# Shared keys and values in the global attention of a hybrid layer, and a shorter neighbourhood chain

## The reference

```python
# 1: neighbourhood attention, 4 heads of 16, window 7x7, then an MLP
x = x + neighbourhood_attention(layernorm(x)) @ proj_w + proj_b     # softmax over 49 keys + rpb
x = x + gelu(layernorm(x) @ fc1_w + fc1_b) @ fc2_w + fc2_b
t = x as (2, 1024, 64)
# 2: global attention, 8 heads of width 64 each, no bias on q, k, v
a = ln(t)
q = (a @ Wq).reshape(b, t, h, e) * e**-0.25
k = (a @ Wk).reshape(b, t, h, e) * e**-0.25
v = (a @ Wv).reshape(b, t, h, e)
t = t + softmax(q k^T) v @ Wu + bu
# 3: a scan of 33 steps; each picks a weight set by an argmax over its state, most do nothing
t = t + scan(ln(t))
```

## Time and profile before

| what | us |
|---|---|
| timed runs | 797.28, 794.80, 792.45 (median 794.8) |
| span of the profiled execution | 796.3 |
| neighbourhood stage, first score to last projection | 26.6 to 177.8 |
| handover | 177.8 to 194.4 |
| global pairs 0, 1, 2, 3 | 106.1, 112.3, 112.2, 102.3 |
| end of pair 3 to the end of the program | 627.3 to 796.3 |
| busy: PE, DVE, ACT, POOL | 679.7, 525.6, 418.5, 30.5 |

### The profile page before, as it was taken

The page is one execution under the profiler, slowest core; times in us unless marked ns, Lnnn a source line. Parts: engine busy times, 40 slices in busy tenths (PEclk is TensorE's granted clock), DMA queues, the critical chain, the costliest instruction groups (busy, mean ns, idle before and its releaser), DMA issues.

```text
span 796.3 us, 11131 instructions
## 1 busy us (share of the span) xinstructions
PE 679.7 (85%) x3779; PEld 355.4 (45%) x3780; DVE 525.6 (66%) x1043; ACT 418.5 (53%) x820; POOL 30.5 (4%) x37
## 2 busy tenths in 40 slices
PE   6899999988779999998998998999999674377862
PEld 4445444644534554554554454554555331144311
DVE  5865685276976767766676677667676645489533
ACT  3543455436666666556566665666666313266330
POOL 4140000000000000000000000000000000000000
PEclk9975555557999999999999999999999895699986
DMA  3000000000000000000000000000000000000001
GB/s 81 1 8 0 2 1 1 1 1 1 0 1 1 1 1 1 1 1 1 1 0 0 0 0 0 0 1 0 2 1 0 1 8 3 11 1 1 1 0 26
DMA packets 9509, 3.22 MB, mean 4 GB/s; under 512 B 8820, under 2 KB 9079, under 8 KB 9463
## 3 DMA queue, kind: packets, MB, share of 16 engines
q1 hardware_dynamic: 8182, 2.61, 1.4%
q10 hardware_dynamic: 1281, 0.01, 0.1%
HBM read 2.09 MB, written 0.52 MB: 3 GB/s over the span
## 4 chain that ended last, share of the span: by engine, by line
PE 69%; DVE 14%; issue 11%; ACT 3%; POOL 1%; DMA 1%; SPq 0%; POOLq 0%; ACTq 0%; DVEq 0%
PE PS L761 13%; PE PS L790 13%; PE PS L774 10%; PE PS L642 5%; PE PS L630 4%; PE PS L718 4%; DVE negm L1527 3%; PE PS L656 3%; DVE kS L1492 2%; PE PS L817 2%; PE PS L483 2%; PE PS L557 2%; PE PS L495 2%; PE PS L507 2%; PE PS L917 1%
## 5 line engine op out<-in xcount | busy, mean ns | idle before, releaser
L1527 DVE TENSOR_REDUCE negm<-PS 128x1 f32<-128x1024 f32 x128 | 156.6, 1223 | 124.7 <-PE PS L761 124.6
L1098 ACT ACTIVATE prob<-PS,negm 128x1024 f32<-128x1024 f32 x128 | 142.7, 1115 | 46.9 <-DVE negm L1527 46.8
L774 PE MATMUL PS<-ident,prob 128*128 128x128 f32 x1024 | 134.6, 274 | 8.4 <-DVE PT L1539 8.3
L790 PE MATMUL PS<-PT,V 128*64 128x512 f32 x512 | 134.3, 617 | 1.9 <-DVE qS L1494 1.9
L774 PEld LDWEIGHTS PS<-ident,prob 128*128 128x128 f32 x1024 | 119.9, 141 | 35.6 <-DVE PT L1539 9.6
L1110 ACT ACTIVATE PT<-PS 128x512 f32<-128x512 f32 x128 | 76.5, 597 | 109.8 <-PE PS L774 109.3
L761 PE MATMUL PS<-kS,qS 128*128 128x512 f16 x512 | 131.8, 380 | 0.0
L1539 DVE COPY PT<-PS 128x512 f32<-128x512 f32 x128 | 87.4, 683 | 5.2 <-PE PS L774 4.4
L761 PEld LDWEIGHTS PS<-kS,qS 128*128 128x128 f16 x512 | 46.0, 98 | 73.3 <-issue 29.2
L1035 ACT ACTIVATE prob<-sbias,negm 128x320 f32<-128x320 f32 (+1 forms) x64 | 34.5, 538 | 43.4 <-DVE negm L1436 43.4
L718 PE MATMUL PS<-aS,wqk 128*128 128x512 f16 x128 | 40.8, 412 | 19.2 <-DVE kS L1492 14.7
(11 more groups left out here) (167 smaller groups left out, 775.8 us busy)
## 6 DMA issues: line engine op xcount, KB each, us to landing
xall<-in_x_dram SPq DMA_DIRECT2D x2, 256.0 KB, 4.3
out_dram<-x SPq DMA_DIRECT2D x4, 128.0 KB, 2.1
w<-in_L_attn_Wq_dram SPq DMA_DIRECT2D x2, 128.0 KB, 2.6
w<-in_L_attn_Wk_dram SPq DMA_DIRECT2D x2, 128.0 KB, 2.8
w<-in_L_attn_Wv_dram SPq DMA_DIRECT2D x2, 128.0 KB, 2.6
fc<-in_L_conv_fc_w_dram SPq DMA_DIRECT2D x2, 64.0 KB, 2.6
wu<-in_L_attn_Wu_dram SPq DMA_DIRECT2D x2, 64.0 KB, 2.4
w1s<-in_L_ffn_ffn_w_dram SPq DMA_DIRECT2D x2, 64.0 KB, 2.1
```

The costliest lines, as they stand in the source:

```text
L774: tr = pe.transpose(bank[:, k * P:(k + 1) * P], prob[:, u % 4, kt * P:(kt + 1) * P], ident[:, :])
L790: mm = pe.matmul(OB[cols, :], V[:, g % GP // 2 * NT + kt, cols], PT[:, g % 2, lane, kt, :], start=(kt == 0), stop=(kt == NT - 1))
L1098: act.activation(prob[:, i % 4, :], scores2[i % 2], ACT.Exp, bias=negm[:, i % 4:i % 4 + 1], scale=1.0, accum_out=sums[:, i // GRP, (i % GR ...
L1527: dve.tensor_reduce(negm[:, i % 4:i % 4 + 1], scores2[i % 2], AX.X, ALU.max, negate=True)\
```

## The change

**Global attention.** Since q k^T = a Wq Wk^T a^T and there is no bias, each head's Wq Wk^T is formed once, and the keys of all heads are the normalised input itself (`aS`, high part in rows 0 to 63, low part in rows 64 to 127); its values are the same input in float32 (`V`, twice side by side, written by `divide(..., twice=True)`), with Wv Wu formed once in place of Wu. `PIECES` keeps only the queries: 32 in all, four ahead of pair 0, eight in pairs 0, 1 and 2 (`common_steps`), four in pair 3. The products are made during the neighbourhood stage: twelve transposes of weights at steps 24 and 27 (`turn_weights`), sixteen float32 matmuls at steps 27 to 33 (`mix_weights`, `fold_values`), six drains on ScalarE, and the split on POOL (`split_weights`) for half as much as before.

**Neighbourhood chain.** The queries carry a minus sign, so bias, mask and the bound are negated and the fused operation yields the negated maximum at once. The row sums come out of the value matmul (a column of ones in `V0`), and the scaling is put behind the projection: `pw0` holds the projection of each head apart and a selector of the sums, so that the projection of a tile is 260 columns wide. VectorE takes four reciprocals and weighs four heads of 64 columns per tile (`weigh_heads`, at step 4T + 9); POOL adds the heads and the residual in four operations per tile (`add_heads`). `nat_turn` waits for the exponential, always turns whole 128x128 chunks, and a drain is one copy. `nat_project` now waits for `weigh_heads` of the tile before.

The core of the diff:

```diff
-LAG_SUM, LAG_DRAIN, LAG_PROJ = 6, 7, 8
+LAG_SUM, LAG_DRAIN, LAG_PROJ, LAG_WEIGH = 6, 7, 8, 9
+YH = 4
-        common_steps = [1, 2, 3, 4, 7, 8, 9, 10, 11, 12] + [16, 17, 18, 19, 20, 24, 25, 26, 27, 28]
+        common_steps = [1, 3, 8, 10] + [17, 19, 24, 26]
-        first_steps = [8, 8, 9, 9, 10, 10, 11, 11, 12, 13] + common_steps[HALF:]
+        first_steps = [8, 9, 10, 11] + common_steps[HALF:]
...
             def nat_turn(u):
-                pe.wait_ge(c0["scaled"], u + 1)
+                pe.wait_ge(c0["exped"], u + 1)
...
-                    tr = pe.transpose(bank[0:k, n * P:(n + 1) * P], prob[:, u % 3, n * P:n * P + k], ident[:, :])
+                    tr = pe.transpose(bank[:, n * P:(n + 1) * P], prob[:, u % 3, n * P:(n + 1) * P], ident[:, :])
...
             def nat_project(T):
-                if T == NT:
-                    pe.wait_ge(c0["y_drained"], 1)
+                if T:
+                    pe.wait_ge(c0["y_drained"], T)
                 pe.wait_ge(c0["out_drained"], T + 1)
-                mm = pe.matmul(YB[:, t * C:(t + 1) * C], OT0[:, T % 2, :], pw0[:, :], start=True, stop=True)
+                pe.matmul(YB[:, 0:NH0 * C + NH0], OT0[:, T % 2, :], pw0[:, :], start=True, stop=True)\
+                  .then_inc(c0["y_filled"], 1)
...
             for n in range(HALF):
-                if n == EARLY:
-                    turn_norm("y", 1, 5)
-                if n >= 4:
-                    pe.wait_ge(piece_drained, n - 3)
-                project(0, n, PS[:, n % 4, :])
+                project(0, n, PS[:, n, :])
+            turn_norm("y", 1, 5)
...
                                 mm = pe.matmul(scores2[i % 2][:, j * BLK:(j + 1) * BLK], qS[:, part, lane, q0:q0 + P],
-                                               kS[:, lane, k0 + j * BLK:k0 + (j + 1) * BLK],
+                                               aS[:, k0 + j * BLK:k0 + (j + 1) * BLK],
...
                     dve.tensor_tensor_reduce(sbias[:, i % 3, 0:w], PS[:, i % 2, 0:w],
...
-                                             1.0, 3 * NEG, ALU.add, ALU.max, maxp[:, i % 4:i % 4 + 1])\
+                                             1.0, -3 * NEG, ALU.add, ALU.min, negm[:, i % 4:i % 4 + 1])\
...
-                    dve.reciprocal(rinv[:, u % 4:u % 4 + 1], rsum[:, u % 4:u % 4 + 1])\
...
-                    dve.tensor_scalar(negm[:, i % 4:i % 4 + 1], maxp[:, i % 4:i % 4 + 1], -1.0, None, ALU.mult)\
...
-                    dve.tensor_scalar(prob[:, u % 3, 0:w], prob[:, u % 3, 0:w], rinv[:, u % 4:u % 4 + 1], None,
-                                      ALU.mult).then_inc(c0["scaled"], 1)
...
+            def weigh_heads(T):
+                dve.wait_ge(c0["y_filled"], T + 1)
+                dve.reciprocal(rinv0[:, T % 2, :], YB[:, NH0 * C:NH0 * C + NH0]).then_inc(c0["inverted"], 1)
+                if T >= YH:
+                    dve.wait_ge(summed, T - YH + 1)
+                dve.wait_ge(c0["inverted"], T + 1)
+                dve.tensor_tensor(yh[:, T % YH], YB[:, 0:NH0 * C].rearrange("p (h c) -> p h c", h=NH0),
+                                  rinv0[:, T % 2, :].rearrange("p (h o) -> p h o", o=1).to_broadcast([P, NH0, C]),
+                                  ALU.mult).then_inc(c0["y_drained"], 1)
...
+            def add_heads(T):
+                pool.wait_ge(c0["y_drained"], T + 1)
+                y, x1 = yh[:, T % YH], xall[:, T, :]
+                link(pool.tensor_tensor(yh2[:, :, :], y[:, 0:2, :], y[:, 2:4, :], ALU.add))
+                pool.sem_inc(summed, 1)
+                link(pool.tensor_tensor(yh1[:, :], yh2[:, 0, :], yh2[:, 1, :], ALU.add))
+                link(pool.tensor_tensor(x1, xb[:, T, :], yh1[:, :], ALU.add))
+                link(pool.tensor_tensor(xb[:, T, :], x1, fb2[:, :], ALU.add))
+                pool.sem_inc(attended, 1)
```

More of the change, by code:

```diff
@@ L797, in glob_pair @@
                             side_wait(pe, ("a", 1, 1))
[L799 to L800 removed]
+                        pe.wait_ge(piece_drained, bp + (HALF + m))
                         g = (i - PROJ - 1) // GRP
@@ L1415, in _ @@
             dve.wait_ge(tables_made, 2 * ROWS)
-            for i in range(UN0 + 3):
+            for i in range(UN0 + LAG_WEIGH - NH0 + 1):
                 if i == (NT - 1) * NH0:
```

265 lines of the change are left out of this document (152 added, 113 removed).

## The result

The changed kernel took 735.33, 745.30, 736.35 and 764.21 us (median 740.8) beside 797.28, 794.80, 792.45 and 795.52 of the kernel before; the ratio is 0.927 (0.922 to 0.931). Predicted were 734 and a range of 709 to 769. Medians are of all executions; the ratios, here and later, leave out those that took over 1.5% longer than the fastest of the same kernel (764.21 here). The profiled execution took 735.33 us, its span is 733.5.

A forecast was written before the change was run, and what follows sets the result against it. TensorE bounds the global stage at full clock and is busy in the neighbourhood stage at clock 0.50. 796.3 - 47 (pieces) + 2 (handover) - 16 (neighbourhood) = 735.3 us profiled, so median 734; range 709 to 769.

The forecast's parts named there:

- Global pieces: Global attention: fewer pieces, at least one step apart, save 47 us over the four pairs, between 35 and 50.
- the other end, 0.90: Pairs 1 and 2: if each piece costs 0.90 us in place of 0.44, they save 10.9 us each, not 14.6.
- no wait for a low part over 0.3 us: Global attention, sign that the forecast holds: no wait of L753 for a low part over 0.3 us.
- Handover: Last projection to first score of pair 0: 2 us lost, between 4 gained and 8 lost.
- The weight work: Neighbourhood stage: twelve transposes and sixteen small float32 matmuls add 10 us at half clock, 5 at full.
- Case A: Neighbourhood stage: 8 of 13.5 tiles at full clock, 16 us saved, 734 us in all; likeliest, chance 0.42.
- the places where the prediction looked for the loss of the clock: Neighbourhood stage: beside six layernorm operations on VectorE (steps 40 to 45, 58 to 63) or the gelu tables on ScalarE.
- C: Neighbourhood stage: half clock throughout, 17 us lost there, 767 us in all; chance 0.27.
- D: Global attention: pieces come back as waits, saving 18 us in place of 47, 763 us in all; chance 0.05.
- E: Neighbourhood stage: POOL's four operations take more than a tile of 7.8 us, 800 us in all; E and F 0.02.
- F: Pair 0 waits for late `split_weights` or folded products; costs nothing unless POOL is as slow as in E; E and F 0.02.
- B: Neighbourhood stage: full clock from step 9 or before nearly to its end, 36 us saved, 714 in all; chance 0.24.

The follow-up runs named there:

- clumped run: Changed kernel with its pieces dealt out at neighbouring steps (1, 2, 3, 4 and 17, 18, 19, 20 of each pair): median 757.9 us (0.948).
- runs of the halves: Each half of the change by itself on the kernel before: global attention median 752.8 us (0.942), neighbourhood chain 785.84 to 805.11 us.
- global half alone: Shared keys and values, 32 pieces and folded weights on the kernel before, with its old neighbourhood chain: median 752.8 us (0.942).
- the narrow one: Changed kernel with the projection of tiles 1 to 15 cut to its last 68 columns, part of the computation left out: median 753.5 us (0.942).
- the repeated one: Changed kernel run again unchanged, on another chip: 745.03 to 756.39 us, median 749.8 (0.939).
- the run with the late split: Kernel before, with POOL's split of the global weights put off until behind step 32 of the neighbourhood stage: 796.5 us (0.996).
- the dense run: Changed kernel with four transposes without use at the end of each of steps 9 to 66 of the neighbourhood stage: 731.65 to 735.10 us (0.919).
- half the filling: Changed kernel with 22 useless matmuls in the handover and two useless transposes at each of steps 12 to 24 and 48 to 66: 713.64 to 739.60 us.

## Why the prediction was right, and where its reasons were not

For the profiled execution 735.3 us were forecast and the span is 733.5. Two errors of the sum nearly cancel in that: the global pieces gave 5.7 us less than forecast (41.3 for 47), the neighbourhood stage 8.4 more (24.4 for 16).

**Global pieces: mechanism right, 41 us in place of 47.** Pairs 1 and 2 gave 13.5 us each for 14, pair 3 5.9 for 6.3. Within the sum it was pair 0 that was mis-sized, 8.4 for 12.6: its steps 8 to 13 take 20.1 us for 18.9, and its first eight, which the prediction left alone, went from 20.0 to 22.6, since two of them now run at half clock (3.28 and 2.97 us). On the whole a piece costs (98.7 - 94.2) / 8 = 0.56 us. The clumped run shows why the other end, 0.90, was not reached: with neighbouring pieces it is (101.9 - 94.2) / 8 = 0.96 again. In pair 0 the pieces of steps 8 to 11 are still neighbours, and there one sign of the prediction, no wait for a low part over 0.3 us, failed: TensorE waits 1.4 us for `aS` and three times 1.1 to 1.3 for `qS`, and these four steps take 3.46 to 3.75 us in place of 3.29.

**Handover: +1.6 for +2**, and the runs of the halves put it to the chain (16.9 us in the global half alone, 19.1 in the other). What the prediction missed is that its idle costs more than itself: through the clock it costs another 6 us behind it.

**Neighbourhood, prices.** A tile at half clock was put at 8.3 us and takes 8.35; the wide projection at 0.55 more, and the narrow one gives 0.54. At full clock 5.7 us were expected and 5.29 came (98.01 to 103.30): the step of 1.01 us, taken from a spell with the old chain, is 0.86 with the new one where TensorE does not wait (101.69 to 102.55), and one wait of 0.46 for VectorE stands in the tile. The first steps were to give 2 us; the first projection starts at 38.07 in place of 40.94, 2.9 earlier. The weight work was put at 5 us at full clock; its rows in the changed kernel sum to 1.91 + 0.60 + 1.10 + 1.10 + 0.68 = 5.4 us, the first of them, ahead of the rise, at half:

```profile
75.10 1.91 PE L596 MATMUL PS<-ident,w 128*128 128x128 f32 x8
...
80.82 0.60 PE L596 MATMUL PS<-ident,w 128*128 128x128 f32 x4
81.35 1.10 PE L608 MATMUL PS<-PT 64*128 64x64 f32 x8
...
86.39 1.10 PE L608 MATMUL PS<-PT 64*128 64x64 f32 x8
...
89.84 0.68 PE L621 MATMUL PS<-wu,PT 64*64 64x64 f32 x16
```

**Neighbourhood, the clock: the weakest step.** Case A had 8 of 13.5 tiles at full clock and 16 us saved. The profiled execution had some nine, 61.4 us, and saved 24.4; the repeated one had 23.9 us at full clock and saved 1.4. The median of the eight runs is 746.6 us, 11.3 above the profiled one; if all of that is this stage, as the starts of the last projection in the two profiles say (23.0 us apart), it saved 13 us in the middle. The forecast hit because that lies near 16, not because the mechanism was understood: the argument was that nothing ends the spell once VectorE's scaling is not held up, and the run with the late split shows that it was not this that ended it. Of the places where the prediction looked for the loss of the clock, at most one was right. It fell at 58.0 us, in step 18, where no loss was forecast; it stayed up beside the layernorm of steps 40 to 45 (96.8 to 104.7 us); and it fell at 122.9, about step 49, beside the gelu tables, whether because of them or not. The layernorm's operations were not held up by POOL's additions either: they take 0.68 to 0.69 us, as before, but for one of 0.94 us beside an addition at 106.5. Cases A and C are two executions of one program, not two answers to one question. The chance for C was well placed; that the same kernel would show both was not seen.

What the dense run adds is a lever on both. Busy as the profile counts it is not what brings or holds the clock: 77.98 of 78.5 us were busy at 0.50. Four transposes of full contraction more in each step gave 1.00 throughout. The Trainium skill, "TensorE: Matmul & The Clock Gate", Part 1, has it that activity releases the throttle. The dense run agrees, if activity is not read as the busy time of a page; by busy time, 0.50 between 89.7 and 168.2 us speaks against it. Whether it is the transposes' 128 rows (the scores have 32) or the gaps that they fill, the runs don't separate. Nor do they show what ends a spell in one execution and not in another of the same program.

**Rivals.** D, pieces back as waits: they come where pieces are neighbours, in pair 0 (three waits for `qS` of 3.6 us in all and one for `aS` of 1.4), and else hardly. E, POOL too slow: its four operations take 0.48 + 0.34 + 0.32 + 0.32 = 1.46 us a tile, far below the 7.8 at which it would decide, and POOL is busy for a quarter of the stage. F: TensorE waits nowhere for the split of the weights. B, full clock nearly throughout, did not come by the change itself but by the filling; it gives 734.6 and not 714. The filling takes TensorE's time, and the handover stays nearly as it was (18.2 us). The one execution of 713.64 us with half the filling would fit B's 714.

## What to carry to other kernels

Where TensorE's clock stands at half although it is busy, removing work from it may give nothing and adding dense work may pay: price a stage at both levels, and treat the level as something the kernel can buy. Idle in front of a dense stage is worth filling, with useful work if there is some. Compare a tile with the same tile, since two neighbours can differ in their number of instructions. Never trust one profile for a stage whose clock changes: look at the starts of known instructions in two executions, and at a duration of a known instruction, before a gain is put down to an edit.

## What the runs showed of the hardware that was not expected

- 232 transposes without use took the kernel from 749.8 (on another chip; 740.8 in its first runs) to 734.6 us, and its scatter from 11 us to 3.5; with 28 matmuls more in the handover to 728.2 and 1.4 us.
- One program got 61.4 us at full clock in one execution of the neighbourhood stage and 23.9 in another, worth 23 us.
- Float32 matmuls of 64 rows ran at full clock for 3.95 us where it was full when they began, and at half for 7.16 where it was not.
- The clock row reads full ahead of the first recorded change, even where the durations are those of half clock.
- VectorE's scalings of 0.34 to 0.39 us took up to 1.78 us beside POOL's split of the weights, and the long ones moved with the split when it was put off by some 50 us. One wait of TensorE of 0.97 us did not end a spell at full clock.
